# The sort's rank product reads its counts from PSUM: VectorE multiplies directly, ScalarE's copy is left out

## The reference

```python
edge_index = jnp.stack([src, dst])
x = _layernorm(x + _L0_gnn_ref(x, edge_index, edge_type_64, ...), axis=-1)
x = _layernorm(x + _L1_gnn_ref(x, src, dst, edge_weight, ...), axis=-1)
x = _layernorm(x + _L2_gnn_ref(x, edge_index, edge_type_2, ...), axis=-1)
x = _layernorm(x + _L3_gnn_ref(x, edge_index, ...), axis=-1)
```

## Time and profile before

| | |
|---|---|
| time, median of 3 runs | 4607.52 us (4606.58 to 4609.63) |
| profiled execution, its own time | 4609.34 us |
| its span | 4607.6 us |
| VectorE busy (DVE) | 4012.2 us, 87% |
| TensorE busy (PE) | 3896.1 us, 85% |
| ScalarE busy (ACT) | 2196.3 us, 48% |
| GpSimd busy (POOL) | 237.3 us, 5% |

### The profile page before, as it was taken

How to read it: one execution, slowest core, us unless ns; L and a number is a source line. 1 busy time by engine, 2 the same in 40 slices (tenths; PEclk the granted TensorE clock), 3 DMA queues, 4 the chain that set the end, 5 groups by cost and what they waited for, 6 DMA issues and landing times. The chain is left out here.

```text
span 4607.6 us, 106894 instructions
## 1 busy us (share of the span) xinstructions
PE 3896.1 (85%) x44112; PEld 3490.5 (76%) x44113; DVE 4012.2 (87%) x6579; ACT 2196.3 (48%) x3936; POOL 237.3 (5%) x165
## 2 busy tenths in 40 slices
PE   3666666666668999995999999997999999979998
PEld 3555555555556666663999999997999999968988
DVE  8999999999998899986999999998666666668888
ACT  2222333333334555552333333333888888857776
POOL 1000001010100000000101110101000000000000
PEclk9899889888879999997999999998999999989999
DMA  3000000000002222221000000000333333300000
GB/s 104 1 1 1 1 1 1 1 1 1 1 1 109 113 113 110 113 110 44 2 2 2 2 2 2 2 2 6 110 96 99 99 97 97 98 12 5 9 10 9
DMA packets 92941, 183.53 MB, mean 40 GB/s; under 512 B 10329, under 2 KB 63781, under 8 KB 92322
## 3 DMA queue, kind: packets, MB, share of 16 engines
q1 hardware_dynamic: 91970, 174.17, 11.6%
q10 hardware_dynamic: 480, 2.40, 0.2%
HBM read 88.63 MB, written 87.90 MB: 38 GB/s over the span
## 5 line engine op out<-in xcount | busy, mean ns | idle before, releaser
L1699 ACT ACTIVATE gC<-qC 128x768 fp32r<-128x768 f32 (+3 forms) x1184 | 981.4, 829 | 802.5 <-PE qC L1740 640.3
L87 DVE TENSOR_TENSOR g<-iota_own,recs 128x768 bf16<-128x768 bf16 (+1 forms) x1200 | 636.4, 560 | 177.0 <-PE qC L1744 171.0
L1846 PE MATMUL qO<-Xr,gC 128*128 128x258 f32 (+1 forms) x4900 | 754.2, 291 | 7.8 <-ACT gC L1699 7.7
L461 PE MATMUL pV<-VO,PM 128*128 128x98 bf16 (+4 forms) x6524 | 400.9, 230 | 409.7 <-issue 404.5
L461 PEld LDWEIGHTS pV<-VO,PM 128*128 128x128 bf16 x6524 | 370.2, 111 | 436.2 <-issue 434.4
L1846 PEld LDWEIGHTS qO<-Xr,gC 128*128 128x128 f32 x4900 | 639.3, 190 | 15.7 <-ACT gC L1699 10.6
L1846 PE MATMUL qO<-A,gC 128*128 128x132 f32 x4900 | 637.2, 281 | 0.0
L1846 PEld LDWEIGHTS qO<-A,gC 128*128 128x128 f32 x4900 | 581.4, 191 | 0.0
L93 DVE TENSOR_TENSOR g<-iota_own,recs 128x1536 bf16<-128x1536 bf16 (+1 forms) x522 | 510.7, 988 | 63.4 <-PE qC L1744 48.3
L1844 PE MATMUL qO<-terms,ring 128*128 128x384 bf16 x2450 | 524.2, 327 | 0.0
L1841 PE MATMUL qO<-terms 128*128 128x64 bf16 x2450 | 470.4, 193 | 0.0
(11 more groups left out here) (248 smaller groups left out, 5709.0 us busy)
## 6 DMA issues: line engine op xcount, KB each, us to landing
sl_f<-tables SPq DMA_DIRECT2D x350, 192.0 KB, 2.3
tables<-ring SPq DMA_DIRECT2D x150, 384.0 KB, 2.3
tables<-ring SPq DMA_DIRECT2D x50, 416.0 KB, 2.4
sl_f<-tables SPq DMA_DIRECT2D x50, 224.0 KB, 2.5
edges<-terms SPq DMA_DIRECT2D x1, 4312.0 KB, 13.4
B<-in_x SPq DMA_DIRECT2D x1, 2744.0 KB
out<-B SPq DMA_DIRECT2D x7, 392.0 KB
terms<-in_edge_type ACTq DMA_DIRECT2D x2, 686.0 KB
```

The source lines that it names most:

```text
L87: return v.tensor_tensor(o.rearrange("p n (a b) -> p n a b", b=2), (iota_own if own else iota_b)[:, at:at + w].rearrange("p (a b) -> p a b ...
L461: mm = pe.matmul(pV[n % 2][:, g * row:(g + 1) * row].rearrange("p (f b) -> p f b", f=u.nf), PM[:, n % 2, col, :], values[:, :, col, :], st ...
L1699: act.activation(Cs[:, u % 2, 0:n, :], pC[u % 2][:, 0:n, :], ACT.Copy).then_inc(s_cs, 1)
L1846: mm = pe.matmul(pO[i % SUMS][:, 0:width], table_j, x, start=first, stop=last)
```

## The change

ScalarE's `looked` is taken out with its tile `R` and its semaphore `s_look`. VectorE's product takes its second input from `pR` itself and waits for TensorE's `s_cnt`. TensorE's `count(n)` waits with `s_mul` for the product of unit n - 2, where it waited for the copy of that unit.

```diff
-            R = sb("R", [P, 2, 512], BF16, c1)
...
-                    def looked(n):
-
-                        u = units[n]
-                        k = u.npos * u.ngrp * u.w
-                        act.wait_ge(s_cnt, n + 1)
-                        if n >= 2:
-                            act.wait_ge(s_mul, n - 1)
-                        act.activation(R[:, n % 2, 0:k], pR[n % 2][:, 0:k], ACT.Copy).then_inc(s_look, 1)
...
-                        looked(a)
                         for n in range(a, b):
                             paired(n)
                             if n > a:
                                 evict(n - 1)
-                            if n + 1 < b:
-                                looked(n + 1)
...
                         if n >= 2:
-                            pe.wait_ge(s_look, n - 1)
+                            pe.wait_ge(s_mul, n - 1)
...
-                            v.wait_ge(s_look, n + 1)
+                            v.wait_ge(s_cnt, n + 1)
                             if n >= 1:
                                 v.wait_ge(s_rank, n)
-                            v.tensor_tensor(M[:, 0:cols * u.w], O[:, n % 2, 0:cols * u.w], R[:, n % 2, 0:cols * u.w], ALU.mult).then_inc(s_mul, 1)
+                            v.tensor_tensor(M[:, 0:cols * u.w], O[:, n % 2, 0:cols * u.w], pR[n % 2][:, 0:cols * u.w], ALU.mult).then_inc(s_mul, 1)
```

More of the change, by code:

```diff
@@ L177, in gnn_four_layers_kernel @@
             names = ("loads", "pads", "consts", "tri_made", "prep", "fields", "blanks", "weighed", "s_pad0", "s_load0", "s_xin0", "s_stored", "turned", "wt_made",
-                     "s_dup", "s_hot", "s_cnt", "s_look", "s_mul", "s_rank", "s_more", "s_pair", "s_val", "s_perm", "s_out", "s_ev",
+                     "s_dup", "s_hot", "s_cnt", "s_mul", "s_rank", "s_more", "s_pair", "s_val", "s_perm", "s_out", "s_ev",
                      "s_outhot", "s_outadd", "s_deg", "s_tp0", "s_xt0", "s_y0", "s_lin0", "s_link0", "s_wt0", "s_valid", "s_total", "s_kind")
             (loads, pads, consts, tri_made, prep, fields, blanks, weighed, s_pad, s_load, s_xin, s_stored, turned, wt_made,
-             s_dup, s_hot, s_cnt, s_look, s_mul, s_rank, s_more, s_pair, s_val, s_perm, s_out, s_ev,
+             s_dup, s_hot, s_cnt, s_mul, s_rank, s_more, s_pair, s_val, s_perm, s_out, s_ev,
              s_outhot, s_outadd, s_deg, s_tp, s_xt, s_y, s_lin, s_link, s_wt, s_valid, s_total, s_kind) = [sem(n, c1) for n in names]
```

## The result

The changed kernel takes 4633.0 us (median of 5 runs, 4631.25 to 4634.01) against 4607.52 (4603.51 to 4610.19): ratio 1.0055, 95% interval 1.0043 to 1.0067. It is 25.5 us slower, where 28.5 were forecast; 4633 lies in the range of 4621 to 4656. The profiled execution has a span of 4631.4 us, 23.8 more than before.

What follows compares the result with a forecast made beforehand. The sort was taken as bound by VectorE. +48.0 for the product, -12.8, -1.6, -2.4 and -3.0 for waits and GpSimd gave +28.2 us, so 4636 us, slower by 0.6%, range 4621 to 4656.

Steps and rivals of the forecast that it cites:

- The bound: The sort is bound by VectorE, busy 417.9 of 419 us in phase 1 and 887.4 of 922 in phase 2.
- The product's price: VectorE's product at line 667, one input now fp32 in PSUM, costs +48.0 us over the sort.
- distances grow by the difference of durations: On busy VectorE the overlap with the next instruction is 0.07 us at either speed, so longer products delay successors equally.
- A fixed price of reading PSUM: None expected: VectorE's sum with pL takes 275 ns, its twin with both inputs in SBUF 281.
- the first rival: The PSUM-reading product loses its overlap or pays a fixed price: 16 us more, 4652; chance 0.14 together with nothing coming back.
- The waits for R: VectorE's 24 waits for ScalarE's copy, 20.5 us, lose 12.8 without the copy; 7.7 are left, for TensorE.
- V and pL: Copies of V and xT no longer queue behind R on ScalarE: -1.6 us ahead of O, -2.4 for product pL.
- GpSimd: Ten products held by GpSimd's line 301 in phase 2 save 0.3 us each, -3.0, bounds 0 and 7.
- The sum: All terms together add 28.2 us, with the sort's end at about 1416 where it was 1388.
- The product at its old speed: Rival: the product from PSUM costs nothing more, so the change gives -17.6 us, 4590, faster; chance 0.04.
- The third rival: Product dearer by about half, or waits and GpSimd give all back and TensorE's clock rises: 4600 to 4619; chance 0.07.
- That nothing comes back: Rival: waits stay as long because TensorE is late by itself, 4656; chance 0.14 together with the lost overlap or fixed price.

Runs made afterwards that it cites:

- e4: The changed kernel without GpSimd's 13 blocks of three instructions in phase 2; 4624.7 us, ratio 1.0033 against the kernel before.
- e6: The kernel before with the product from PSUM in the 177 units of phase 2 only; 4623.9 us, ratio 1.0037.
- e3: The kernel before without GpSimd's 13 blocks of three instructions in phase 2; 4600.8 us, ratio 0.9979.
- e5: The kernel before with the product from PSUM in the 49 units of phase 1 only; 4618.6 us, ratio 1.0022.
- the first seven experiments: Runs with fp32 copy, copy kept beside a PSUM product, both kernels without GpSimd's blocks, each phase alone, ScalarE's queue reordered; 4600.8 to 4656.2 us.
- e2: The kernel before, VectorE still waiting for ScalarE's copy but multiplying with the counts in PSUM; 4653.0 us, ratio 1.0087.

## Why the prediction was right, point by point

**The bound.** Right: VectorE is busy 430 of 431 and 918 of 938 us after, and what its product costs reaches the end. ScalarE's busy time fell by 111.7 us, to 2084.6, and the time rose all the same.

**The product's price.** Forecast +48.0; measured 47.0 by the undisturbed distances. That is midway between the two neighbours between which I chose, the reduction (45.7) and the fp32 sum from PSUM (48.3). The step that distances grow by the difference of durations held: 0.53 and 0.47 to the successor, as forecast.

**A fixed price of reading PSUM.** Right to leave it out. The same product takes 619 ns with its counts in PSUM and 623 with them as fp32 in SBUF, and its successor starts 0.531 and 0.535 us behind it. That leaves no room for the 0.07 us a product of the first rival.

**The waits for R.** Forecast -12.8 with 7.7 left, measured -11.8 with 8.7 left. The sum was right, one of its two parts wasn't. The copy's own 0.53 is right. "M of the unit before is 0.20 to 0.24 longer, which pushes the time at which VectorE is ready into the wait" is wrong as a saving of its own: with the longer product and the copy kept, the waits stayed at 20.4 and 19.4. What makes up for it seems to be the clock, which I had held fixed while changing the pace of the unit. In these two runs, the changed kernel and the two other runs whose phase 2 multiplies from PSUM without filling (e4 and e6), it is 0.85 to 0.86 from 480 us on, and 56 to 63 of some 170 counts are slow; in before, e3 and e5, with the short product there, it is 0.87 with 50 to 53 slow counts.

**V and pL.** Forecast -1.6 and -2.4. pL gave 2.3. V gave about 5, 4 of it in the products of 392 elements and 1 in those of 448, since most of its waits sit inside the distance from M to O; the idle column shows only what reaches beyond the overlap, and that is all I had counted.

**GpSimd.** Forecast -3.0 with 7 as the bound; 6.1 by the profiles, not settled by the medians. The mechanism is shown: the product is no longer held (0.55 us where it was 1.07 in the same place), another instruction is. VO costs 4.7 us more; without GpSimd it takes 125.6 us in the changed kernel, as before.

**The sum.** 47.0 - 11.8 - 5 - 2.3 - 6.1 = 21.8, and 1.0 less for the start of phase 2, where O no longer waited for V, against 20.7 measured in the sort; +28.2 was forecast for it, with the sort's end at 1416 where it came at 1409. Of the 7.5 us too many, about 3.4 are V's, 3.1 GpSimd's, 1.0 the product's and 1.0 the start of phase 2; the waits for R, overrated on the other side, take 1.0 off. Some 3 us of the 23.8 lie outside the sort, which I had at nothing. Between its end and the end of the span the profiles of before and of the first seven experiments vary from 3220 to 3228 us, so 2.5 us there can be no more than the ordinary spread; its cause stays open. So the time came nearer to the forecast (25.5 for 28.5) than the sort did (20.7 for 28.2), and that is luck: 3.1 us outside the sort and 1.7 between the profiled executions and the medians filled part of the gap.

**The rivals.** The product at its old speed and the fixed price are out. The third rival had the clock rise with VectorE's slower pace; it fell, from 0.87 to 0.85. That nothing comes back is out for the change as it stands, and nearly true (45.0 of 47.0) where the filling has removed the waits by other means.

## What to carry to other kernels

Count what a removed copy frees in waits, not in busy time: 226 copies of 0.5 us on ScalarE were worth 20 us, and the slower rate of the reader behind them cost 41 to 47 (a product of 448 elements took 374 ns with both inputs in bf16, 602 with the counts in PSUM). When the engine that reads has no gaps, let the idle one convert to bf16 in SBUF. And before a wait is engineered away, see why its producer is late: here ten matmuls of no use in an idle gap of TensorE took 28.7 us off the sort where leaving out the copy was worth 20.4, and without its price.

## What the runs showed of the hardware

In these runs TensorE's granted clock over a stretch was higher where its idle time was filled, and the time of a kernel whose sort VectorE bounds went down as it rose. With the same work on VectorE the clock from 480 us to the sort's end went from 0.87 to 0.99 when ten matmuls (1.26 us in the unit shown) were added in each unit, and the time fell by 0.46%. The same thirteen matmuls of a count take 2.33 us in the earlier trace rows, in a count with a granted clock of 0.50, and 1.27 at 701.05 above, in one with 1.00. One fall in the kernel before, in TensorE's rows:

```profile
631.34 1.27 PE L445 MATMUL pR<-O,ones_b 128*128 128x364 bf16 x13
636.35 1.35 PE L461 MATMUL pV<-VO,PM 128*128 128x96 bf16 x28 [3.74 <-issue]
637.54 0.37 PE L442 MATMUL pR<-O,tri_b 128*128 128x392 bf16 x1
637.70 2.33 PE L445 MATMUL pR<-O,ones_b 128*128 128x364 bf16 x13
```

TensorE stood idle for 3.74 us ahead of 636.35; the granted clock was 1.00 from 631 to 634 us and is 0.54 from 637.5 to 640. With ten filling matmuls a unit TensorE's idle gaps of over 0.15 us, from 480 us to the sort's end, come to some 180 us where they were 308. The low clock comes behind this wait, but not at once: the burst at 636.35 still runs fast (28 matmuls in 1.35 us, a granted clock of 1.00 from 636.35 to 637.54), and the count behind it is the slow one. Whether the wait is what brings the clock down, no run tests by itself. That the drop from 0.87 to 0.85 is what kept the waits up in the runs with the longer product is inferred from this, not tested by itself.

GpSimd's `terms` instruction held a VectorE product that reads two SBUF tensors until it had finished (before, 576.12: 1.07 us instead of 0.36) and let one pass that reads its second input from PSUM (e2, 592.85: 0.55 us). Freeing one instruction here moved the hold to the next one with two SBUF inputs: of the 6.9 us that GpSimd cost at M (43.6 against 36.7 without it), 4.7 came back at VO.
